# Finer waits ahead of the matmuls of the linear layers, six dummy matmuls fewer at the head, and the square roots of layer L0 moved up

## What is computed

```python
# block L0
styles = w @ (affine_w * gain).T + affine_b
dcoefs = rsqrt(sum((weight * styles) ** 2, axis=2) + 1e-08)
y = einsum('blc,oc->blo', x * styles, weight) * dcoefs
x = x + clip(y + bias, -256, 256)
# block L1: modulated_linear is the same pattern with its own style and demod
kx = modulated_linear(x, s, k_aff_w, k_aff_b, k_w, k_b)      # "K"; q = k = v = kx
A = softmax(einsum('bnhd,bnjd->bnhj', kx, kx) / sqrt(32))    # 16 heads against 16 heads, per token
out = einsum('bnhj,bnjd->bnhd', A, kx).reshape(B, N, F)
x = x + modulated_linear(out, s, o_aff_w, o_aff_b, o_w, o_b) # "O"
```

## Time and profile before

| | us |
|---|---|
| median of 3 runs | 695.31 |
| lowest and highest of them | 694.22, 699.59 |
| the profiled execution's own time | 695.16 |
| its span, first to last instruction | 693.3 |
| PE busy in the span | 683.5 |
| DVE busy | 582.0 |
| ACT busy | 542.7 |

### The profile page before, as it was taken

One profiled execution on the slowest core, in us unless ns is written; L12 is line 12 of the kernel. 1 busy time (PEld: TensorE's weight loads), 2 busy tenths in 40 slices (PEclk: granted clock), 3 DMA queues, 4 the chain that ended last, 5 costly groups with the idle time before them and its releaser, 6 DMA issues.

```text
span 693.3 us, 21691 instructions
## 1 busy us (share of the span) xinstructions
PE 683.5 (99%) x8900; PEld 666.8 (96%) x8900; DVE 582.0 (84%) x1057; ACT 542.7 (78%) x1070; POOL 119.6 (17%) x109
## 2 busy tenths in 40 slices
PE   9999999999999999999999999999999999999988
PEld 8999999999999999899999999999999999999878
DVE  4689987889888899788888888898888898888785
ACT  6898977888777888778887778887778887788683
POOL 2022311222102222012222012222012221012311
PEclk9999999999999999999999999999999999999999
DMA  9377878488877778777678767788776688776857
GB/s 307 120 188 196 224 191 237 149 223 214 196 201 193 204 215 213 204 177 197 202 202 219 200 172 215 206 211 204 193 209 201 198 214 206 192 205 195 230 139 236
DMA packets 230099, 140.37 MB, mean 202 GB/s; under 512 B 141425, under 2 KB 223857, under 8 KB 230001
## 3 DMA queue, kind: packets, MB, share of 16 engines
q1 hardware_dynamic: 228528, 138.73, 73.6%
q10 hardware_dynamic: 1472, 0.27, 0.2%
HBM read 71.85 MB, written 67.11 MB: 200 GB/s over the span
## 4 chain that ended last, share of the span: by engine, by line
PE 68%; ACT 11%; DMA 8%; DVE 5%; SPq 4%; issue 3%; DVEq 0%; ACTq 0%; POOL 0%; POOLq 0%
PE lin_ps L505 54%; PE y_ps L575 6%; PE s_ps L557 5%; DMA yr<-y_turned 4%; DMA k_turned<-kx 3%; ACT p_bd L704 2%; DMA y_turned<-y 2%; ACT y_hi L608 2%; SPq L318 2%; ACT kx L599 2%; ACT x_hi L608 1%; SPq L294 1%; SPq L310 1%; DVE x L882 1%; PE s_ps L515 1%
## 5 line engine op out<-in xcount | busy, mean ns | idle before, releaser
L505 PE MATMUL lin_ps<-x_hi,w_hi 128*128 128x256 f32 x1024 | 287.5, 284 | 0.4
L505 PE MATMUL lin_ps<-x_lo,w_hi 128*128 128x256 f32 x1024 | 281.9, 279 | 0.0
L505 PE MATMUL lin_ps<-x_hi,w_lo 128*128 128x256 f32 x1024 | 281.7, 279 | 0.0
L460 POOL COPY k_bd<-k_rhs 32x1024 f32<-32x1024 f32 x94 | 110.5, 1176 | 538.3 <-DVE k_rhs L861 534.7
L505 PEld LDWEIGHTS lin_ps<-x_hi,w_hi 128*128 128x128 f32 x1024 | 190.9, 188 | 9.0 <-issue 7.2
L505 PEld LDWEIGHTS lin_ps<-x_lo,w_hi 128*128 128x128 f32 x1024 | 190.8, 188 | 0.0
L505 PEld LDWEIGHTS lin_ps<-x_hi,w_lo 128*128 128x128 f32 x1024 | 190.8, 188 | 0.0
L608 ACT ACTIVATE x_hi<-x,style 128x256 fp32r<-128x256 f32 x256 | 114.9, 502 | 59.7 <-DVE x L882 59.2
L801 DVE SCALAR_TENSOR_TENSOR x_lo<-x,style,x_hi 128x256 fp32r<-128x256 f32 x256 | 146.8, 625 | 13.4 <-ACT x_hi L608 13.4
L505 PE MATMUL lin_ps<-y_hi,w_hi 128*128 128x256 f32 x512 | 144.6, 282 | 0.0
L505 PE MATMUL lin_ps<-y_lo,w_hi 128*128 128x256 f32 x512 | 144.0, 281 | 0.0
(11 more groups left out here) (67 smaller groups left out, 733.6 us busy)
## 6 DMA issues: line engine op xcount, KB each, us to landing
k_st<-k_turned SPq DMA_DIRECT2D x128, 128.0 KB, 3.2
v_turned<-k_rhs SPq DMA_DIRECT2D x32, 512.0 KB, 6.0
k_v<-v_turned SPq DMA_DIRECT2D x128, 128.0 KB, 3.6
y_turned<-y SPq DMA_DIRECT2D x126, 128.0 KB, 3.3
x<-xT SPq DMA_DIRECT2D x31, 512.0 KB, 5.9
k_turned<-kx SPq DMA_DIRECT2D x30, 512.0 KB, 3.0
yr<-y_turned SPq DMA_DIRECT2D x29, 512.0 KB, 4.8
outT<-o SPq DMA_DIRECT2D x29, 512.0 KB, 4.2
```

The costliest lines, as they stand in the source:

```text
L460: pool.tensor_copy(k_bd[HD * r:HD * (r + 1), r], k_rhs[HD * r:HD * (r + 1)]).then_inc(g_kbd, 1)
L505: mm = pe.matmul(lin_ps[:, (n + j) % NLB, 0:T], w[:, k, (m + j) * P:(m + j + 1) * P], r[:, k, :], start=(k == 0 and q == 0), stop=(k == KB ...
```

## The change

Three edits:

1. In `linear` the waits are put at the first matmul that reads what is waited for: x_hi and w_hi ahead of product 0, x_lo ahead of product 1, w_lo ahead of product 2. The same values are waited for as before.
2. The 4 dummies ahead of the first slices of L0 are left out, and 4 instead of 6 stand between the two halves of `styles(L0)`.
3. On ACT, `roots(L0)` and the wait for its small constant come ahead of x_hi of the second half of chunk 1 instead of behind it.

```diff
@@ -57,7 +57,7 @@
-    WARM_STYLES, WARM_HALF, WARM_L0 = 8, 6, 4
+    WARM_STYLES, WARM_HALF = 8, 4
@@ -213,7 +213,7 @@
         pe_program = (
-            [("warm", WARM_STYLES), ("styles", L0, 0), ("warm", WARM_HALF), ("styles", L0, 1), ("warm", WARM_L0)]
+            [("warm", WARM_STYLES), ("styles", L0, 0), ("warm", WARM_HALF), ("styles", L0, 1)]
             + [("lin", L0, 0, 0, KB, 0, 3)] + one("norms", L0) + [("lin", L0, 0, 0, KB, 3, KB), ("styles", K)]
@@ -491,14 +491,18 @@
                 for k in range(first, end):
-                    if m == 0 and k in (0, KB // 2):
-                        h = k // (KB // 2)
-                        pe.wait_ge(split[l][0], 2 * c + h + 1)
-                        pe.wait_ge(split[l][1], 2 * c + h + 1)
-                    if m == 0 and c == 0 and k * parts[l] % KB == 0:
-                        pe.wait_ge(a_whi, split_done(l, k * parts[l] // KB))
-                        pe.wait_ge(v_wlo, split_done(l, k * parts[l] // KB))
+                    new_data = m == 0 and k % (KB // 2) == 0
+                    new_weights = m == 0 and c == 0 and k * parts[l] % KB == 0
+                    raised = 2 * c + k // (KB // 2) + 1
                     for q, (w, r) in enumerate(((w_hi[l], hi), (w_hi[l], lo), (w_lo[l], hi))):
+                        if q == 0 and new_data:
+                            pe.wait_ge(split[l][0], raised)
+                        if q == 0 and new_weights:
+                            pe.wait_ge(a_whi, split_done(l, k * parts[l] // KB))
+                        if q == 1 and new_data:
+                            pe.wait_ge(split[l][1], raised)
+                        if q == 2 and new_weights:
+                            pe.wait_ge(v_wlo, split_done(l, k * parts[l] // KB))
                         for j in range(width):
@@ -646,9 +650,9 @@
             weights_squared(L0)
             x_hi_of(1, 0)
-            x_hi_of(1, 1)
             act.wait_ge(g_eps, 1)
             roots(L0)
+            x_hi_of(1, 1)
             act.wait_ge(ld_small, DMA * SMALL)
```

## The result

| | before | after |
|---|---|---|
| median of 20 runs each, us | 695.65 | 700.59 |
| lowest to highest | 691.64 to 701.40 | 697.37 to 705.54 |
| ratio, with its 95% interval | | 1.0061 (1.0041 to 1.0082) |
| the profiled execution's own time (span) | 695.16 (693.3) | 697.48 (695.7) |

The forecast was 0.84 us less; measured is 4.2 us more (0.0061 x 695.65; 2.9 to 5.7 us). The execution that was profiled after is one of the fastest of its kind.

The account below looks back on a forecast made before the run. The prediction took the kernel to be bound by TensorE's own work through its long middle. It summed 0.72 us at the head and 0.12 at the end to 0.84, from 695.31 to 694.5 us, range 692.5 to 696.9.

Parts of the forecast that it names:

- The dummies: Head: removed dummies save 0.51 and 0.92 us; the second affine load does not hold PE; L0 starts at 7.15.
- What is late next: Head: `norms(L0)` waits for ACT's squared weights until 12.11, starting at 12.24 instead of 12.96, a gain of 0.72 us.
- the stall at 21 to 22 us: K's first four matmuls wait for banks ACT evacuates late; the stall stays as long and the 0.72 us pass through.
- The roots: ACT at the head: roots start at 13.45, avoiding 0.26 us; the move is hidden, at worst 0.1 us lost.
- From there to the middle: From the head into the loop: the 0.72 us pass through; 192 new wait places in the middle are booked at 0.
- the first of the rivals: Middle: new waits break the stream of weights, 192 places x 0.07 = 13.4 us slower, 708 us; chance 2%.
- a head that is earlier with a span that isn't: Sign in the profile after: head earlier by 0.7 us but span not, putting the error in the passage to the middle.
- The end: K's first block in the last chunk: the finer wait gains 0.12 us, between 0 and 0.19.
- The late clock at the head: Head: PE's stalls keep the lower clock until `norms`, 3.6 us longer less 0.4, giving 697.7; chance 4%.
- The head's gain does not arrive: At 22.6 us and after: ACT's evacuation row or a load sets the time, which stays at 695.3; chance 20%.
- The 1%: Whole kernel: the least difference a measurement can tell from no change, about 1%, 7 us.

Follow-up runs that it names:

- after head good: Whole change plus 64 satisfied waits at the head and 114 in L0 of chunks 6, 12, 18 and 24, against before: ratio 0.9975, median 693.46 us.
- after again: The whole change run and profiled a second time, nothing else altered, against before: ratio 1.0060, span of the profiled execution 699.5 us.
- after padded: Whole change with always satisfied waits put back ahead of slice 2 of each first block (294 semaphore instructions), against before: ratio 1.0014.
- after good: Whole change plus 118 satisfied waits in L0, placed so no 256-instruction boundary falls near the end of scores in the loop, against before: ratio 1.0005.
- waits only: Only the waits moved to the first matmul reading each operand, dummies and roots as before, against the kernel before: ratio 1.0075.
- lean: Kernel before without the redundant wait for the hi part of the data, 97 fewer semaphore instructions on PE, against before: ratio 1.0044.
- before plus: Kernel before with two more satisfied waits ahead of slice 2 of each first block, 398 semaphore instructions, against before: ratio 0.9992.
- after headpad: Whole change plus 64 satisfied waits in L0 of chunk 3 and K of chunk 1, against before: ratio 1.0010.
- before good: Kernel before plus 256 satisfied waits in L0 of six chunks, placed to remove its one late instruction load, against before: ratio 1.0006.

## Why the prediction was wrong, point by point

- **The dummies**, right in this trace: PE reached L0 at 6.93, forecast 7.15, since the first eight dummies ended some 0.3 us earlier in that execution. The stall ahead of product 1 ended at 7.85, forecast 7.94. But "so it does not hold PE", of the second affine load, fails: with fewer dummies PE waits for it, 0.3 us in after and 1.0 in after head good. The load lands anywhere from 6.15 to 7.26 us over the 19 traces, and `norms` starts at 12.11 to 12.66 in six of the seven traces of the whole change and its padded forms, and at 13.05 in the seventh, after head good.
- **What is late next**, right: the squares set `norms`, at 12.11, forecast 12.24. The head gained 0.84 us, forecast 0.72, and it passed the stall at 21 to 22 us unchanged, as said. That the size fits is in part luck: after again gained 0.40.
- **The roots**, right: the roots ran at 13.31 (forecast 13.45), the evacuation at 14.54 (14.66).
- **From there to the middle**, wrong, and this is the step that failed. "Since no wait is open there when PE comes, I book 0" is true of each wait, and the pace of an undisturbed pass did not change. What I left out is that a wait is an instruction too. The sentence counted 192 places and no instructions, so it missed that 101 of 302 go away (and 24 more with the dummies) and that the loads of PE's program, in blocks of 256 instructions, fall elsewhere after it. The runs showed in its place a loss that goes with the count and place of instructions and not with the place of the waits: 97 instructions fewer alone cost 0.44%, and 64 put back at the head bring 1.0060 down to 1.0010. The bound "no gain; the loss is the first of the rivals" was no bound: it looked only at the place of the wait. The prediction's own sign for this case, a head that is earlier with a span that isn't, points at the right passage.
- **The end**: at K's last block PE was 0.25 us ahead at matmul 8144 and 0.53 at 8214, so the finer wait gave some 0.3 us there, more than the 0.12 forecast. It was gone by 8543, where the chain of transfers was 0.4 us later than before.
- **The rivals.** The first had the right edit and the right sign with a wrong mechanism: the stream of weights is not broken, since after padded and after good, with the same finer waits, are at 1.0014 and 1.0005. The late clock at the head did not come. "The head's gain does not arrive" comes nearest, but it named ACT's evacuation row or a load, at 22.6 us and after, and a time that stays; what gave the gain back are 1.8 and 2.3 us in pass 5, at 88 to 108 us, where an instruction load meets the y load and DVE's product meets POOL's copy.
- **The size.** The two profiled executions of after are 4.5 us longer than the two of before on average, near the 4.2 of the runs. By stretches: -0.6 us up to matmul 1043 (the head), +2.0 from there to 1280 (pass 5), +0.5 to 8213 (the loop), +2.6 to the end (60.7 against 58.1). The loop's part is within the scatter: against before it is -1.2 us in one execution and +2.7 in the other, and their late loads there, 2.1 and 1.8 us, are no more than the 1.6 and 1.9 of before. How the loss splits over executions that were not profiled stays open. In waits only, whose pass 5 loses nothing, the late loads alone are 6.5 us, so as much time can be lost at quite other places.
- **The range** of 692.5 to 696.9 was made of terms seen in one trace. The 20 runs of before go from 691.64 to 701.40, and a term of some us that hangs on coincidences between queues should have widened it. The 1% that the prediction took for the least that can be told was too wide in turn: with 20 runs each the interval is 0.2% to either side, 1.4 us, which shows the loss, and still would not have shown a gain of 0.84 us.

## What to carry to other kernels

An edit that adds or removes instructions on a long unrolled engine moves every later load of its program; a difference of some tenths of a per cent that no wait of the change explains should be tried against the same kernel with instructions added that do nothing, before the edit itself is praised or blamed. Where a stretch uses up its instructions far faster than the rest (here 256 in 3.6 us), look for waits named "issue" at its end and for loads of the instruction queue beside them. And a transfer on the critical chain can be late by 2 us beside such a load: 6.6 instead of 4.7 us here, and 4.7 again once the load was moved.

## What the runs showed of the hardware that I had not expected

- Instruction loads of 16 KB, each 0.9 to 2.2 us long, can reach PE late when a block begins within 8 matmuls of the end of a stretch of 256 instructions in 3.6 us: in 31 of 54 cases, 1.4 us a time, up to 2.8.
- Such a stall can bring the lower clock in the middle of the kernel, but need not: it followed stalls in lean, waits only and before plus, and did not follow the longest, of 2.8 us in after headpad. Windows of lean: length, busy us (records) of PE, PEld, DVE, ACT, POOL, granted clock, DMA. In lean no matmul had started for 2.1 us, from 152.85 to 154.93; then the clock is 0.50, 1.2 GHz, and the matmuls start 0.21 us apart instead of 0.12:

```profile
152.00:155.50 3.50, 1.70 (x34) 1.29 (x23) 1.57 (x4) 3.05 (x7) 0.00 (x0) 1.00 0.39 137
155.70:159.00 3.30, 3.30 (x17) 3.30 (x17) 1.51 (x3) 1.08 (x2) 0.00 (x0) 0.50 0.40 100
```

- Satisfied waits cost PE nothing that shows: 96 more semaphore instructions gave 0.9992, and 256 more (before good) 1.0006; the whole change with 178 more (after head good) is at 0.9975.
- An engine's instruction can take twice as long by starting 0.2 us later beside another engine's: DVE's product took 0.69 us when it began just ahead of POOL's copy and 1.50 to 1.54 just behind it.
